# Software-pipelining the prefix state update of a gated linear attention kernel over (chunk, head) items

## The chip, the cores and the metric

The kernel runs on all 8 cores of one Trainium2 chip. The cores do not exchange data. The metric is the device time in microseconds (us) of the slowest core.

## The reference

One transformer layer: gated linear attention (GLA), then a mixture-of-experts FFN, each between a layer norm and a normed residual. The change touches the GLA only, cut here to its core (B = 2, S = 8192, D = 1024, H = 8, DK = 128, DV = 256):

```python
q, k, v = x @ Wq, (x @ Wk) * DK ** (-0.5), x @ Wv          # per head
alpha = sigmoid((x @ Wg + bg) / 16.0)                        # one per token and head
def step(state, inp):
    state = at[..., None, None] * state + kt[..., None] * vt[:, :, None, :]
    out_t = jnp.einsum('bhk,bhkv->bhv', qt, state)
out = outs * sigmoid(x @ Wog) @ Wo
```

## The kernel before

**Split.** Each core owns 2048 tokens of one batch row. The state at the first of them depends on all tokens before, so each core first runs a *prefix* of 6144 tokens (filled up with zeros where fewer exist) that only builds the state, and then the mixer for its own tokens, and then the FFN. All cores do the same amount of work.

**Prefix** (`emit_prefix`). 12 super-tiles of 512 tokens, each with: the load of `x_tm` (issued by SyncE once the previous super-tile's gate work is done), layer norm and transposes (VectorE, ScalarE, TensorE), the K and V projections (long rows of matmuls into banks 2 and 3), the gate (`emit_gproj`, `emit_gateprep`, which end with `Rxb` and `Rxm`, the exponentials of running sums of log alpha), and then the state updates: 4 chunks of 128 tokens x 8 heads = 32 *items* (c, h), in that order, one call of `emit_state_update` each. That makes 12 x 32 = 384 items.

**One item i** has seven steps. The letters are used throughout; `par` is h % 2 and picks one of two SBUF buffers.

- B(i), TensorE: two matmuls that spread the head's row of `Rxb` and `Rxm` over 128 partitions, into bank 6 (`pb<-Rxb,isel8b` and `pb<-Rxm,isel8b`)
- K(i), VectorE, L536: `khb` = k times the second of them
- E(i), ScalarE, L541: `expB`, one column of the first (the decay of the chunk)
- T(i), TensorE: transpose of `khb` into bank 7 (`pb<-iI128b,khb`)
- C(i), ScalarE, L547: copy of it to SBUF, `khT`
- S(i), TensorE: the state's increment, `khT` x `v_tm`, into another part of bank 7 (`pb<-v_tm,khT`)
- A(i), VectorE, L555: `S_state` = `S_state` x `expB` + bank 7

**What sets the order.** Each engine runs its instructions in the order of the program, and waits at semaphores that the helpers place. `mm` (start of a group in a bank) waits until all readers recorded for that bank have finished, whatever part of the bank they read; `pbread` (a read of a bank) waits for the last sealed matmul of that bank, and enters itself as a reader. `opi` on VectorE and ScalarE adds a wait for that engine's own previous instruction. A wait that an earlier, later-counting wait on the same semaphore already covers is left out (`Bld.wait`). All matmuls are issued by L158, in `mm`.

Of the kernel before, what the change touches and what calls it, by code (L numbers as in the profile page):

```python
# [11 lines left out]
ALU = mybir.AluOpType  # L12
# [3 lines left out]
H, DK, DV, D, HDV = 8, 128, 256, 1024, 2048  # L16
C = 128
# [130 lines left out]
def mm(b, pb, out, lhsT, rhs, start, stop, seal=False):  # L148
    if start:
        assert not pb.open, "interleaved accumulation groups in one PSUM bank"  # L150
        for tok in pb.rtoks:
            b.wait("t", tok)
        pb.rtoks = []
        pb.open = True
    if stop:
        pb.open = False
    pb.unsealed = True
    fn = lambda E, o=out, l=lhsT, r=rhs, st=start, sp=stop: E.matmul(  # L158
        o, l, r, start=st, stop=sp)
    if seal:  # L160
        pb.wtok = b.opi("t", fn)
        pb.unsealed = False
    else:
        b.op("t", fn)


def pbread(b, pb, e, fn):
    assert not pb.unsealed, "reading PSUM bank with unsealed writes"
    b.wait(e, pb.wtok)
    tok = b.opi(e, fn)  # L170
    pb.rtoks.append(tok)
    return tok
# [34 lines left out]
def _build(cfg, dma_plan):  # L207
# [51 lines left out]
    b = Bld(nc, es, dma_plan)  # L259
    _dbgn = [0]  # L260

    def dkey():
        _dbgn[0] += 1
        return "dbg%d" % _dbgn[0]
# [3 lines left out]
    pb = [PB(es.enter_context(nc.psum_tensor(f"pb{i}", [128, 512], F32)))  # L268
          for i in range(8)]
    iI128b = sb("iI128b", [128, 128], BF16)  # L270
    iones1b = sb("iones1b", [1, 128], BF16)
    iones2b = sb("iones2b", [2, 128], BF16)
    CCm = TS // C
    expB_rd = [None, None]
# [31 lines left out]
    isel8b = msb("isel8b", [8, 8 * 128], BF16)  # L306
    imask = msb("imask", [128, 128], F32)
    S_state = msb("S_state", [128, H * DV], F32)
# [7 lines left out]
    Rxb = msb("Rxb", [8, TS], BF16)  # L316
    Rxm = msb("Rxm", [8, TS], BF16)
# [5 lines left out]
    khb = [msb(f"khb{p}", [128, 128], BF16) for p in range(2)]  # L323
    khT = [msb(f"khT{p}", [128, 128], BF16) for p in range(2)]
    Sbf = [msb(f"Sbf{p}", [128, DV], BF16) for p in range(2)]
    expB_sb = [msb(f"expB{p}", [128, 1], F32) for p in range(2)]
    outog = msb("outog", [128, 16, 128], BF16)
    xln_fm = msb("xln_fm", [128, 8, TS], BF16)
    k_fm = msb("k_fm", [128, H, TS], BF16)
    v_tm = msb("v_tm", [128, CCm, H * DV], BF16)  # L330
# [24 lines left out]
    def emit_ln1(x_src_3d, cc, st_off=0):  # L355
        o = st_off
        for j in range(cc):
            sqb = sqbuf[j % 2]
            b.opi("v", lambda E, j=j: E.reduce_sum(  # L359
                st_s1[:, o + j:o + j + 1], x_src_3d[:, j, :], axis=AX.X))  # L360
            b.wait("s", sq_rd[j % 2])
            tsq = b.opi("s", lambda E, j=j, sqb=sqb: E.activation(
                sqb[:, :], x_src_3d[:, j, :], AF.Square))
            b.wait("v", tsq)
            sq_rd[j % 2] = b.opi("v", lambda E, j=j, sqb=sqb: E.reduce_sum(  # L365
                st_sq[:, o + j:o + j + 1], sqb[:, :], axis=AX.X))
        b.wait("s", b.tok("v"))
        b.opi("s", lambda E, o=o, cc=cc: E.mul(
            st_mean[:, o:o + cc], st_s1[:, o:o + cc], 1.0 / D))
        tmsq = b.opi("s", lambda E, o=o, cc=cc: E.activation(  # L370
            st_msq[:, o:o + cc], st_mean[:, o:o + cc], AF.Square))
        b.wait("v", tmsq)
        tvar = b.opi("v", lambda E, o=o, cc=cc: E.scalar_tensor_tensor(
            st_var[:, o:o + cc], st_sq[:, o:o + cc], 1.0 / D, st_msq[:, o:o + cc],
            ALU.mult, ALU.subtract))
        b.wait("s", tvar)
        b.wait("s", tk_eps)
        b.op("s", lambda E, o=o, cc=cc: E.activation(
            st_msq[:, o:o + cc], st_var[:, o:o + cc], AF.Ln,
            bias=ieps[:, :], scale=1.0))  # L380
        tkr = b.opi("s", lambda E, o=o, cc=cc: E.activation(
            st_rstd[:, o:o + cc], st_msq[:, o:o + cc], AF.Exp, bias=0.0, scale=-0.5))
        b.wait("v", tkr)
        tmr = b.opi("v", lambda E, o=o, cc=cc: E.scalar_tensor_tensor(
            st_mr[:, o:o + cc], st_mean[:, o:o + cc], -1.0, st_rstd[:, o:o + cc],
            ALU.mult, ALU.mult))
        b.wait("s", tmr)
        return tmr
# [137 lines left out]
            Rxm[:, 0:cc * C], ts2[:, 0:cc * C], AF.Exp, bias=0.0, scale=1.0))  # L526
        return tkR, None

    def emit_state_update(c, h, par, tkR, v_tok):
        bank6 = pb[6]  # L530
        b.wait("t", tkR)
        mm(b, bank6, bank6.sl(par * 256, 128), isel8b[:, h * 128:(h + 1) * 128],
           Rxb[:, c * C:(c + 1) * C], start=True, stop=True)
        mm(b, bank6, bank6.sl(par * 256 + 128, 128), isel8b[:, h * 128:(h + 1) * 128],
           Rxm[:, c * C:(c + 1) * C], start=True, stop=True, seal=True)
        tkh = pbread(b, bank6, "v", lambda E, bank6=bank6, par=par, c=c, h=h: E.tensor_tensor(  # L536
            khb[par][:, :], k_fm[:, h, c * C:(c + 1) * C],
            bank6.sl(par * 256 + 128, 128), ALU.mult))
        b.wait("s", expB_rd[par])
        b.wait("s", tkh)  # L540
        tEB = pbread(b, bank6, "s", lambda E, bank6=bank6, par=par: E.copy(  # L541
            expB_sb[par][:, :], bank6.sl(par * 256 + 127, 1)))
        bank7 = pb[7]
        b.wait("t", tkh)
        mm(b, bank7, bank7.sl(par * 128, 128), khb[par][:, :], iI128b[:, :],
           start=True, stop=True, seal=True)
        tkt = pbread(b, bank7, "s", lambda E, bank7=bank7, par=par: E.copy(  # L547
            khT[par][:, :], bank7.sl(par * 128, 128)))
        b.wait("t", tkt)
        if v_tok is not None:  # L550
            b.wait("t", v_tok)
        mm(b, bank7, bank7.sl(256, 256), khT[par][:, :],
           v_tm[:, c, h * DV:(h + 1) * DV], start=True, stop=True, seal=True)
        b.wait("v", tEB)
        tadd = pbread(b, bank7, "v", lambda E, bank7=bank7, par=par, h=h: E.scalar_tensor_tensor(  # L555
            S_state[:, h * DV:(h + 1) * DV], S_state[:, h * DV:(h + 1) * DV],
            expB_sb[par][:, :], bank7.sl(256, 256), ALU.mult, ALU.add))
        expB_rd[par] = tadd
        return tadd

    x_cons = [None]
    x_par = [0]
# [1 line left out]
    def emit_prefix():  # L564
        for s in range(n_pre_st):
            if x_cons[0] is not None:
                b.wait("y", x_cons[0][0])
                b.wait("y", x_cons[0][1])
            tkx = b.dma("y", x_tm[:, :, :],
                        x_pre.rearrange("(a p) n -> p a n", p=128)[:, s * CCm:(s + 1) * CCm, :],  # L570
                        "x%d" % (x_par[0] % 2))
            x_par[0] += 1
            b.wait("v", tkx)
            b.wait("s", tkx)
            emit_ln1(x_tm, CCm)
            for j in range(CCm):
                tkn = emit_norm_sub(x_tm, j, xlnbuf[j % 2])
                emit_transpose_to_fm(xlnbuf[j % 2], xln_fm, tkn, j * 128)
            tk_fmdone = b.tok("s")
            x_cons[0] = (b.tok("v"), b.tok("s"))  # L580
            if cfg.micro < 2:
                continue
            b.wait("t", tk_fmdone)
            b.wait("t", tk_wk)
            b.wait("t", tk_wv)
            b.wait("t", tk_wg)
            def kev(bank, i, n0, nn):
                pbread(b, bank, "v", lambda E, bank=bank, i=i, n0=n0, nn=nn: E.tensor_copy(
                    k_fm[:, i, n0:n0 + nn], bank.sl(0, nn)))
            proj_fm_resident(k_fm, Wk_sb, H, TS, kev, scale_tok=tk_wks)  # L590
            v_tok = emit_vproj(CCm, TS)
            if cfg.micro < 3:
                x_cons[0] = (b.tok("v"), b.tok("s"))
                continue
            tk_la = emit_gproj(CCm, TS)
            x_cons[0] = (b.tok("v"), b.tok("s"))
            if cfg.micro < 4:
                continue
            tkR, _ = emit_gateprep(CCm, tk_la)
            x_cons[0] = (b.tok("v"), b.tok("s"))  # L600
            if cfg.micro < 8:
                continue
            for c in range(CCm):
                for h in range(H):
                    emit_state_update(c, h, h % 2, tkR, v_tok)
        if cfg.debug:
            tkf = b.tok("v")
            b.wait("y", tkf)
            tdS = b.dma("y", dbg["dbg_S"][:, :], S_state[:, :], dkey())
            for _e in ("t", "v", "s"):  # L610
                b.wait(_e, tdS)
# [201 lines left out]
    def emit_ffn():  # L813
# [308 lines left out]
        ffn_es.close()  # L1122

    emit_prefix()
    pre_es.close()
    if cfg.stop_after != "prefix":
# [120 lines left out]
```

How the kernel before makes its waits and increments, by code:

```python
    def opi(self, e, fn):  # L76
        h, n = self.sem[e]
        if e in self.AUTO_SER and n > self.waited[e].get(e, 0):
            self.waited[e][e] = n
            self.emit(e, lambda E, h=h, c=n: E.wait_ge(h, c))
        self.sem[e][1] += 1
        self.emit(e, lambda E, fn=fn, h=h: fn(E).then_inc(h, 1))
        return (e, self.sem[e][1])
# [4 lines left out]
    def wait(self, e, tok):  # L88
        if tok is None:
            return
        pe, cnt = tok
        if pe == e and e not in self.AUTO_SER:
            return
        if self.waited[e].get(pe, 0) >= cnt:
            return
        self.waited[e][pe] = cnt
        h = self.sem[pe][0]
        self.emit(e, lambda E, h=h, c=cnt: E.wait_ge(h, c))
# [3 lines left out]
    def dma(self, qe, out, in_, skey):  # L102
        if skey not in self.sem:
            self._mksem(skey)
            self.dma_keys.add(skey)
        idx = self.dma_calls.get(skey, 0)
        self.dma_calls[skey] = idx + 1
        amt = 16
        if self.dma_plan is not None:
            amt = self.dma_plan[skey][idx]
        self.sem[skey][1] += amt
        h = self.sem[skey][0]
        self.emit(qe, lambda E, o=out, i=in_, h=h: E.dma_start(
            out=o, in_=i).then_inc(h, 16))
        return (skey, self.sem[skey][1])
```

## Time and profile before

| | us |
|---|---|
| runs shown | 7725.72 and 7847.7 (median 7786.71) |
| profiled execution, device time | 7743.92 |
| its span, first to last instruction, slowest core (core 3) | 7742.4 |
| spans of the eight cores | 7695.7 to 7742.4 |
| core 3: TensorE busy | 4506.5 (58%) |
| core 3: VectorE busy | 2088.2 (27%) |
| core 3: ScalarE busy | 1576.8 (20%) |

The profile is one execution, seen on the slowest core. On core 3 the prefix ends near 1982 us, the core's own tokens near 3800 us, and the FFN takes the rest. Busy shares are averages over these parts. In the timelines, each line is one instruction: start, duration, engine, line, operation, and in brackets how long the engine was idle before it and what released it.

### The profile page before, as it was taken

What the parts mean: (1) busy time and instruction counts of PE and PEld (TensorE: products, weight loads), DVE (VectorE), ACT (ScalarE), POOL (GpSimd) and SP (SyncE); (2) the same over time, 40 slices, a digit from 0 to 9 for tenths busy, and PEclk for the clock granted to TensorE, in tenths of its full rate; (3) what the DMA queues carried; (4) which work ended last, traced back from release to release, by engine and by line L of the source; (5) the groups of instructions that cost most, each with busy time, mean ns of one, the idle gap of its engine ahead of it and who ended that gap; (6) DMA issues with size and microseconds to landing.
All of it is one profiled execution on the core that took longest, in us unless ns stands there. A gap on an engine that the chain in (4) does not pass through costs nothing.

```text
span 7742.4 us, 71715 instructions; the slowest of 8 cores (7695.7 to 7742.4 us)
## 1 busy us (share of the span) xinstructions
PE 4506.5 (58%) x21600; PEld 2075.7 (27%) x21600; DVE 2088.2 (27%) x4478; ACT 1576.8 (20%) x3527; POOL 246.9 (3%) x300
## 2 busy tenths in 40 slices
PE   3455444554544535454305777777777777778880
PEld 1122221222221212222102333333333333334440
DVE  2333333333222232322342122222222222221113
ACT  1221222212122111212221122222222222221112
POOL 0000000000100001000000000000000000000000
PEclk8667666666666757576557899999999999999985
DMA  2000000000411304031003111111211111112102
GB/s 55 11 11 12 22 11 11 11 11 11 63 22 30 33 20 44 9 40 21 27 25 46 22 22 22 22 22 26 37 26 22 22 22 22 22 22 44 22 1 84
DMA packets 265487, 200.18 MB, mean 26 GB/s; under 512 B 142020, under 2 KB 224068, under 8 KB 265110
## 3 DMA queue, kind: packets, MB, share of 16 engines
q0 software_dynamic: 244448, 128.23, 12.7%
q1 hardware_dynamic: 20662, 67.36, 2.5%
q8 instruction: 183, 3.00, 0.2%
q14 instruction: 194, 1.59, 0.1%
HBM read 307.00 MB, written 16.78 MB: 42 GB/s over the span
## 4 chain that ended last, share of the span: by engine, by line
PE 54%; ACT 15%; DVE 13%; issue 11%; DMA 5%; ACTq 1%; DVEq 1%; POOL 0%; POOLq 0%; SPq 0%
PE pb L158 54%; ACT h_sc L1041 4%; DVE S_state L555 2%; ACT cwb_sb L1023 2%; DVE st_sq L365 2%; DVE st_s L359 2%; DMA wog_buf<-Wog 2%; DVE khb L536 1%; ACT khT L547 1%; ACT xln_fm L406 1%; DMA wq_buf<-Wq 1%; DMA wk_buf<-Wk 1%; ACT Sbf L750 1%; DMA y<-y_sb 1%; ACT xlnB L391 1%
## 5 line engine op out<-in xcount | busy, mean ns | idle before, releaser
L158 PE MATMUL pb<-x1ln_fm,w1g 128*128 128x384 bf16 (+1 forms) x7680 | 1354.6, 323 | 728.3 <-ACT h_sc L1041 408.6
L158 PE MATMUL pb<-w2g,h_sc 128*128 128x512 bf16 x5120 | 1202.2, 387 | 8.9 <-DVE h_sc L1048 8.9
L158 PEld LDWEIGHTS pb<-x1ln_fm,w1g 128*128 128x128 bf16 x7680 | 681.0, 101 | 1348.8 <-issue 1036.3
L1048 DVE TENSOR_TENSOR h_sc<-h_sc,cwb_sb 128x384 bf16<-128x384 bf16 (+1 forms) x768 | 258.1, 336 | 2029.6 <-ACT h_sc L1041 1987.9
L1041 ACT ACTIVATE h_sc<-pb,b1T_sb 128x384 bf16<-128x384 f32 (+1 forms) x768 | 420.1, 547 | 1323.7 <-PE pb L158 1323.7
L158 PEld LDWEIGHTS pb<-w2g,h_sc 128*128 128x128 bf16 x5120 | 506.9, 100 | 592.5 <-issue 71.7
L1082 DVE TENSOR_TENSOR acc<-acc,pb 128x512 f32<-128x512 f32 x640 | 439.9, 687 | 669.2 <-PE pb L158 614.9
L158 PE MATMUL pb<-Wv_sb,xln_fm 128*128 128x512 bf16 x2048 | 444.6, 379 | 0.0
L1023 ACT CAST cwb_sb<-pb 128x384 bf16<-128x384 f32 (+1 forms) x384 | 170.7, 445 | 963.4 <-PE pb L158 924.5
L158 PE MATMUL pb<-v_tm,khT 128*128 128x256 bf16 x512 | 189.2, 370 | 289.1 <-ACT khT L547 217.2
L555 DVE SCALAR_TENSOR_TENSOR S_state<-S_state,expB,pb 128x256 f32<-128x256 f32 x384 | 184.3, 480 | 587.2 <-PE pb L158 587.2
L158 PE MATMUL pb<-iI128b,khb 128*128 128x128 bf16 x512 | 141.9, 277 | 335.7 <-DVE khb L536 335.7
L158 PE MATMUL pb<-iI128b,xlnA 128*128 128x128 bf16 x320 | 40.5, 306 | 489.2 <-ACT xlnA L391 489.2
L158 PEld LDWEIGHTS pb<-Wv_sb,xln_fm 128*128 128x128 bf16 x2048 | 200.2, 98 | 241.8
L462 DVE CAST v_tm<-pb 128x512 bf16<-128x512 f32 x256 | 177.1, 692 | 264.9 <-PE pb L158 264.9
L158 PE MATMUL pb<-smb,v_tm 128*128 128x128 bf16 x256 | 61.1, 288 | 305.2 <-ACT Sbf L750 305.2
L158 PE MATMUL pb<-xln_fm,Wk_sb 128*128 128x512 bf16 x768 | 199.1, 428 | 14.0 <-ACT xln_fm L406 14.0
L541 ACT COPY expB<-pb 128x1 f32<-128x1 f32 x384 | 61.8, 161 | 674.5 <-DVE khb L536 658.2
L1041 ACT ACTIVATE h_sc<-pb,sb1T_sb 128x384 bf16<-128x384 f32 (+1 forms) x192 | 105.0, 547 | 455.4 <-PE pb L158 451.8
L158 PE MATMUL pb<-xln_fm,wog_buf 128*128 128x512 bf16 x512 | 142.1, 432 | 91.2 <-DMA wog_buf<-Wog 86.0
L158 PE MATMUL pb<-cwT,selg 64*128 64x384 bf16 (+1 forms) x384 | 126.5, 329 | 97.0 <-DVE selg L1007 70.9
L158 PEld LDWEIGHTS pb<-iI128b,khb 128*128 128x128 bf16 x512 | 58.8, 115 | 426.8 <-issue 426.8
(145 smaller groups left out, 3757.0 us busy)
## 6 DMA issues: line engine op xcount, KB each, us to landing
w1g<-w POOLq DMA_DIRECT2D x64, 512.0 KB, 13.8
w2g<-w POOLq DMA_DIRECT2D x64, 512.0 KB, 15.6
x_tm<-x_pre SPq DMA_DIRECT2D x12, 2048.0 KB, 9.0
wog_buf<-Wog POOLq DMA_DIRECT2D x64, 256.0 KB, 4.4
x_tm<-x_own SPq DMA_DIRECT2D x4, 2048.0 KB, 7.6
wq_buf<-Wq POOLq DMA_DIRECT2D x32, 256.0 KB, 5.2
wk_buf<-Wk POOLq DMA_DIRECT2D x32, 256.0 KB, 5.1
x_sp<-x_tm SPq DMA_DIRECT2D x16, 512.0 KB, 2.6
```

The costliest lines, as they stand in the source:

```text
L158: fn = lambda E, o=out, l=lhsT, r=rhs, st=start, sp=stop: E.matmul(o, l, r, start=st, stop=sp)
L359: b.opi("v", lambda E, j=j: E.reduce_sum(st_s1[:, o + j:o + j + 1], x_src_3d[:, j, :], axis=AX.X))
L365: sq_rd[j % 2] = b.opi("v", lambda E, j=j, sqb=sqb: E.reduce_sum(st_sq[:, o + j:o + j + 1], sqb[:, :], axis=AX.X))
L391: return b.opi("s", lambda E, j=j, dst=dst: E.activation(dst[:, :], x_src_3d[:, j, :], AF.Identity, bias=st_mr[:, st_off + j:st_off + j + ...
L406: pbread(b, bank, "s", lambda E, bank=bank, half=half: E.copy(dst_fm[:, half * 4:half * 4 + 4, tslice0:tslice0 + 128], bank.t[:, 0:512].re ...
L462: pbread(b, bank, "v", lambda E, bank=bank, c=c, cb4=cb4: E.tensor_copy(v_tm[:, c, cb4 * 512:(cb4 + 1) * 512], bank.t[:, 0:512]))
L536: tkh = pbread(b, bank6, "v", lambda E, bank6=bank6, par=par, c=c, h=h: E.tensor_tensor(khb[par][:, :], k_fm[:, h, c * C:(c + 1) * C], ban ...
L555: tadd = pbread(b, bank7, "v", lambda E, bank7=bank7, par=par, h=h: E.scalar_tensor_tensor(S_state[:, h * DV:(h + 1) * DV], S_state[:, h * ...
L1023: lambda E, bankh=bankh, par=par, tscnt=tscnt: E.copy(cwb_sb[:, par, 0:tscnt], bankh.sl(0, tscnt)))
L1041: dst=dst, tscnt=tscnt: E.activation(dst[:, par, hc, 0:tscnt], bankh.sl(0, tscnt), AF.Silu, bias=bias_ap, scale=1.0))
L1048: b.op("v", lambda E, par=par, hc=hc, tscnt=tscnt: E.tensor_tensor(h_sc[:, par, hc, 0:tscnt], h_sc[:, par, hc, 0:tscnt], cwb_sb[:, par, 0: ...
L1082: lambda E, bank=bank, g128=g128, half=half: E.tensor_tensor(acc[:, g128, half * 512:(half + 1) * 512], acc[:, g128, half * 512:(half + 1) ...
```

## The change

`emit_state_update` is replaced by `emit_prefix_scan`, which emits the 32 items of a super-tile together, in three groups of steps: `front(i)` = B, K, E; `mid(i)` = T, C; `back(i)` = S, A. Round i of the loop emits front(i), then mid(i-1), then back(i-2). So each engine's program order in a round becomes

- TensorE: B(i), T(i-1), S(i-2)
- VectorE: K(i), A(i-2)
- ScalarE: E(i), C(i-1)

After the last round come mid(31), back(30), back(31). The banks, the two buffers of `khb`, `khT` and `expB`, and every instruction's operands are the same as before. `khb_rd` is a new guard: K(i) waits for T(i-2). E(i) is ordered after A(i-4) and not after A(i-2), so that the `expB` buffer of item i-2 is written again before A(i-2) reads it.

```diff
-    def emit_state_update(c, h, par, tkR, v_tok):
-        (B, K, E, T, C, S, A of one item, in this order)
+    khb_rd = [None, None]
+
+    def emit_prefix_scan(cc, tkR, v_tok):
+        bank6, bank7 = pb[6], pb[7]
+        seq = [(c, h) for c in range(cc) for h in range(H)]
+        st_f = {}
+        def front(i):
+            c, h = seq[i]
+            par = i % 2
+            b.wait("t", tkR)
+            mm(b, bank6, bank6.sl(par * 256, 128), isel8b[:, h * 128:(h + 1) * 128],
+               Rxb[:, c * C:(c + 1) * C], start=True, stop=True)
+            mm(b, bank6, bank6.sl(par * 256 + 128, 128), isel8b[:, h * 128:(h + 1) * 128],
+               Rxm[:, c * C:(c + 1) * C], start=True, stop=True, seal=True)
+            b.wait("v", khb_rd[par])
+            tkh = pbread(b, bank6, "v", ...khb...)
+            b.wait("s", expB_rd[par])
+            b.wait("s", tkh)
+            tEB = pbread(b, bank6, "s", ...expB_sb...)
+            st_f[i] = (tkh, tEB)
+        def mid(i):
+            par = i % 2
+            tkh, tEB = st_f[i]
+            b.wait("t", tkh)
+            mm(b, bank7, bank7.sl(par * 128, 128), khb[par][:, :], iI128b[:, :],
+               start=True, stop=True, seal=True)
+            khb_rd[par] = ("t", b.sem["t"][1])
+            tkt = pbread(b, bank7, "s", ...khT...)
+            st_f[i] = (tkt, tEB)
+        def back(i):
+            c, h = seq[i]
+            par = i % 2
+            tkt, tEB = st_f.pop(i)
+            b.wait("t", tkt)
+            if v_tok is not None:
+                b.wait("t", v_tok)
+            mm(b, bank7, bank7.sl(256, 256), khT[par][:, :],
+               v_tm[:, c, h * DV:(h + 1) * DV], start=True, stop=True, seal=True)
+            b.wait("v", tEB)
+            tadd = pbread(b, bank7, "v", ...S_state...)
+            expB_rd[par] = tadd
+        n = len(seq)
+        for i in range(n):
+            front(i)
+            if i >= 1:
+                mid(i - 1)
+            if i >= 2:
+                back(i - 2)
+        if n >= 1:
+            mid(n - 1)
+        if n >= 2:
+            back(n - 2)
+        if n >= 1:
+            back(n - 1)
...
-            for c in range(CCm):
-                for h in range(H):
-                    emit_state_update(c, h, h % 2, tkR, v_tok)
+            emit_prefix_scan(CCm, tkR, v_tok)
```

## Rows read from the trace of the kernel before

**Rows 1.** The page: its head, the busy line, the granted clock.

```profile
span 7742.4 us, 71715 instructions; the slowest of 8 cores (7695.7 to 7742.4 us)
...
PE 4506.5 (58%) x21600; PEld 2075.7 (27%) x21600; DVE 2088.2 (27%) x4478; ACT 1576.8 (20%) x3527; POOL 246.9 (3%) x300
...
PEclk8667666666666757576557899999999999999985
```

**Rows 2.** Busy time by stretch: state updates, the work between them, state updates again.

```profile
core 3: us, PE busy (x) PEld busy (x) DVE busy (x) ACT busy (x) POOL busy (x), PEclk, DMA share, GB/s
...
139.00:216.50 77.50, 30.63 (x128) 10.63 (x128) 24.57 (x64) 14.76 (x65) 0.00 (x0) 0.50 0.08 28
216.50:300.00 83.50, 52.43 (x242) 24.97 (x242) 29.86 (x44) 19.08 (x26) 0.00 (x0) 0.77 0.00 1
300.00:377.00 77.00, 30.28 (x126) 10.50 (x126) 24.58 (x65) 14.79 (x66) 0.00 (x0) 0.50 0.08 28
```

**Rows 3.** Chain of work by time, 302.4 to 308: start, duration, what.

```profile
304.38 0.49 DVE S_state L555
304.87 0.03 issue
304.90 0.02 DVEq L80
304.92 0.04 issue
304.97 0.30 DVE khb L536
305.27 0.14 issue
305.40 0.28 PE pb L158
```

**Rows 4.** Timeline of one item and the start of the next.

```profile
304.97 0.29 DVE L536 TENSOR_TENSOR khb<-k_fm,pb 128x128 bf16<-128x128 bf16 x1
...
305.40 0.27 PE L158 MATMUL pb<-iI128b,khb 128*128 128x128 bf16 x1 [0.89 <-DVE khb L536]
305.45 0.16 ACT L541 COPY expB<-pb 128x1 f32<-128x1 f32 x1 [1.77 <-DVE khb L536]
305.81 0.27 ACT L547 CAST khT<-pb 128x128 bf16<-128x128 f32 x1 [0.20 <-PE pb L158]
...
306.23 0.37 PE L158 MATMUL pb<-v_tm,khT 128*128 128x256 bf16 x1 [0.56 <-ACT khT L547]
...
306.53 0.28 PE L158 MATMUL pb<-Rxb,isel8b 8*128 8x128 bf16 x1
...
306.61 0.31 PE L158 MATMUL pb<-Rxm,isel8b 8*128 8x128 bf16 x1
306.77 0.48 DVE L555 SCALAR_TENSOR_TENSOR S_state<-S_state,expB,pb 128x256 f32<-128x256 f32 x1 [1.51 <-PE pb L158]
307.35 0.29 DVE L536 TENSOR_TENSOR khb<-k_fm,pb 128x128 bf16<-128x128 bf16 x1
```

**Rows 5.** Instructions that write khT and expB over the whole run.

```profile
L547 ACT CAST khT<-pb x384: 266/267/267, 140.5 to 1979.7; 128x128 bf16<-128x128 f32 x192
...
L541 ACT COPY expB<-pb x384: 161/161/162, 140.2 to 1979.3; 128x1 f32<-128x1 f32 x192
```

**Rows 6.** Timeline, own tokens: ScalarE's next instruction behind the expB copy.

```profile
2188.53 0.16 ACT L745 COPY expB<-pb 128x1 f32<-128x1 f32 x1 [1.51 <-DVE khb L740]
2188.78 0.41 ACT L750 CAST Sbf<-S_state 128x256 bf16<-128x256 f32 x1
```

**Rows 7.** Timeline where a super-tile's state updates begin.

```profile
139.12 0.26 PE L158 MATMUL pb<-Rxb,isel8b 8*128 8x128 bf16 x1 [1.30 <-ACT Rxm L525]
...
139.66 0.29 DVE L536 TENSOR_TENSOR khb<-k_fm,pb 128x128 bf16<-128x128 bf16 x1 [1.46 <-PE pb L158]
```

**Rows 8.** Timeline where they end and the next layer norm begins.

```profile
375.81 2.21 ACT L362 ACTIVATE sq<-x_tm 128x1024 f32<-128x1024 f32 x2
...
376.41 0.48 DVE L555 SCALAR_TENSOR_TENSOR S_state<-S_state,expB,pb 128x256 f32<-128x256 f32 x1 [1.51 <-PE pb L158]
376.99 1.22 DVE L359 TENSOR_REDUCE st_s<-x_tm 128x1 f32<-128x1024 f32 x1
```

**Rows 9.** Timeline of an item with a late khT copy.

```profile
322.11 0.27 PE L158 MATMUL pb<-iI128b,khb 128*128 128x128 bf16 x1 [0.87 <-DVE khb L536]
322.16 0.16 ACT L541 COPY expB<-pb 128x1 f32<-128x1 f32 x1 [1.76 <-DVE khb L536]
322.58 0.27 ACT L547 CAST khT<-pb 128x128 bf16<-128x128 f32 x1 [0.25 <-PE pb L158]
```

More of the change, by code:

```diff
@@ L527, in emit_gateprep @@
         return tkR, None
-    def emit_state_update(c, h, par, tkR, v_tok):
[L530 to L559, printed above, removed]
@@ new lines, in _build @@
+    khb_rd = [None, None]
[12 more added lines that the diff above has]
+            b.wait("v", khb_rd[par])
+            tkh = pbread(b, bank6, "v", lambda E, par=par, c=c, h=h: E.tensor_tensor(
+                khb[par][:, :], k_fm[:, h, c * C:(c + 1) * C],
+                bank6.sl(par * 256 + 128, 128), ALU.mult))
+            b.wait("s", expB_rd[par])
+            b.wait("s", tkh)
+            tEB = pbread(b, bank6, "s", lambda E, par=par: E.copy(
+                expB_sb[par][:, :], bank6.sl(par * 256 + 127, 1)))
+            st_f[i] = (tkh, tEB)
[6 more added lines that the diff above has]
+            khb_rd[par] = ("t", b.sem["t"][1])
+            tkt = pbread(b, bank7, "s", lambda E, par=par: E.copy(
+                khT[par][:, :], bank7.sl(par * 128, 128)))
+            st_f[i] = (tkt, tEB)
[9 more added lines that the diff above has]
+            b.wait("v", tEB)
+            tadd = pbread(b, bank7, "v", lambda E, par=par, h=h: E.scalar_tensor_tensor(
+                S_state[:, h * DV:(h + 1) * DV], S_state[:, h * DV:(h + 1) * DV],
+                expB_sb[par][:, :], bank7.sl(256, 256), ALU.mult, ALU.add))
+            expB_rd[par] = tadd
[12 more added lines that the diff above has]
+            back(n - 1)
```

## Prediction

> **What bounds the kernel now.** I read the page first. TensorE is busy 58% of the span and no other engine reaches 30% [rows 1], and the granted clock is low through the first half. So the prefix is not at the rate of any engine, and the busy shares say nothing about the change. Next I cut the prefix into stretches [rows 2]. The state updates of a super-tile fill a stretch of about 77 us in which TensorE is busy 30 us, VectorE 25 us and ScalarE 15 us, at a granted clock of 0.50 (the 1.2 GHz level). Between two such stretches the clock averages 0.77. Twelve stretches of 77 us are some 920 us, 12% of the span: this is all that the change touches. No engine is full in it, so latency sets it.
>
> The chain of waits shows which latency [rows 3], and the timeline gives each step [rows 4]. K starts at 304.97 and the next K at 307.35: one item takes 2.38 to 2.40 us; I use 2.39. From start to start the hand-overs in the loop are:
>
> - A(i-1) to K(i): 304.38 to 304.97, 0.59 (the VectorE instruction of 0.48 and 0.11 for the wait on itself)
> - K(i) to T(i): 304.97 to 305.40, 0.43
> - T(i) to C(i): 305.40 to 305.81, 0.41
> - C(i) to S(i): 305.81 to 306.23, 0.41 to 0.42
> - S(i) to A(i): 306.23 to 306.77, 0.55
>
> Their sum is 2.39. All seven steps lie in one line except E (305.45 to 305.61, beside T) and B (306.53 to 306.92, beside A). The durations of the two ScalarE steps do not vary over 384 items [rows 5]. At the end of the stretch the next layer norm starts on VectorE 0.58 after the last A began [rows 8], while ScalarE has gone ahead. So the end of the last A sets when the next stage begins, and what the stretch loses the run loses.
>
> **The change, step by step.** Nothing is removed: the same seven steps of each item run, on the same two banks. What changes is who stands behind whom. I follow a steady round from the start of S(i-2), with what stands ahead of each instruction:
>
> 1. A(i-2) needs S(i-2): +0.55.
> 2. K(i+1) is next on VectorE and waits for its own engine: +0.59 more. Its B(i+1) was issued behind S(i-2), 0.31 to 0.69 after its start as in [rows 4], and is done in time.
> 3. E(i+1) starts 0.48 after K(i+1) (304.97 to 305.45 [rows 4]). Its three waits are the ones it has now.
> 4. T(i) needs bank 7 free of A(i-2), and K(i) long done. VectorE to TensorE takes 0.14 [rows 3], so T(i) starts 0.62 after A(i-2) began, at about the time K(i+1) starts. It is ready for C(i) at 0.62 + 0.41 = 1.03 after A(i-2) began.
> 5. C(i) stands behind E(i+1) on ScalarE. E(i+1) starts 0.59 + 0.48 = 1.07 after A(i-2), takes 0.16, and then comes ScalarE's wait on itself. Before, that hand-over is hidden, since T ends later. The nearest row is on the core's own tokens, where the same 0.16 us copy is followed at once by another ScalarE instruction: 2188.53 + 0.16 to 2188.78 is 0.09 [rows 6]. So C(i) starts at 1.07 + 0.16 + 0.09 = 1.32, not at 1.03. T is off the path with 0.29 to spare.
> 6. S(i-1) needs bank 7 free of C(i), which is the reader just entered, although its own operand C(i-1) has been ready for a round: +0.41.
>
> The round is 0.55 + 0.59 + 0.48 + 0.25 + 0.41 = 2.28 us. Before it was 0.55 + 0.59 + 0.43 + 0.41 + 0.41 = 2.39. The whole gain of a round is that E with its hand-overs (0.48 + 0.25 = 0.73) takes the place of T with its own (0.43 + 0.41 = 0.84): 0.11 us. The three-deep order on paper overlaps nothing else, because bank 7 is shared by T, C, S and A, and `mm` waits for every reader of the bank.
>
> Filling and draining have to be paid once per super-tile. I count from K(0), which starts 0.54 after B(0) [rows 7] in both kernels.
>
> Before: A(31) starts at 31 x 2.39 + 0.43 + 0.41 + 0.42 + 0.55 = 75.9 and ends at 76.4. (The stretch shown ran from 300.17 to 376.89, 76.7; the rest is scattered late issues such as [rows 9], which I leave alike in both.)
>
> After: E(0) ends at 0.64; B(1) must wait for it (0.14), and K(1) follows at 0.78 + 0.54 = 1.32. By the same step K(2) starts at 2.64, E(2) at 3.12, C(1) at 3.37, S(0) at 3.78, A(0) at 4.33. Then 29 rounds of 2.28: A(29) starts at 70.45. The tail: T(31) at +0.62 = 71.07, C(31) 71.48, S(30) 71.89, A(30) 72.44, then S(31) again at +0.62 = 73.06, A(31) 73.61, ended 74.1.
>
> 76.4 - 74.1 = 2.3 us for each super-tile, and 12 x 2.3 = 27 us. The profiled execution took 7743.9 us, so the forecast is **7716.5 us**, 0.35% less. The runs of before shown have a median 43 us above their profiled execution (0.6%), more than the whole effect. What a comparison of this kernel can tell from no change is about 2%.
>
> *Costs at nothing.* TensorE gets two more waits per item (B now waits for K of the item before, S for two copies in place of one). Both are met before the instruction ahead has finished, so they lie under S and under C. A met wait costs about 0.06 in the chain (0.02 and 0.04 [rows 3]); if the cover were gone, 2 x 0.06 x 384 = 46 us would turn the gain into a loss of 19 us. The new guard on `khb` and the one on `expB` emit nothing, as later waits on the same semaphores cover them. No DMA is moved: the load of the next x tile is issued by SyncE before the first item and is not on this chain. If E were late, C, S, A and the next K behind it all move.
>
> *A page on this.* The Trainium skill says in PSUM — Partial Sum Buffer, "PSUM bank collisions raise a hardware error", that two engines must not touch one bank in the same partitions at once, other columns or not, so that semaphores should guard whole banks. That is a rule against the overlap the new order seems to offer. It agrees with the trace, where T, C, S and A follow each other strictly.
>
> **The rivals.**
>
> *Bank 7 alone sets the round.* If C did not queue behind E (say E started much earlier than it does now), the loop would be T 0.41, C 0.41, S 0.55, A 0.62 = 1.99 us. That is 0.29 less than 2.28, over 29 rounds and 12 super-tiles 101 us more gained: 7616 us. Against it: E(i+1) is emitted before C(i), ScalarE runs in order, and E cannot start before K. Chance 0.03.
>
> *Full overlap.* If the items really overlapped three deep, TensorE would be the bound with 0.28 + 0.31 + 0.27 + 0.37 = 1.23 us an item [rows 4]. 384 x (2.39 - 1.23) = 445 us: 7298 us, 5.7% less. For it: TensorE is busy only 30 of 77 us [rows 2]. Against it: the bank's readers, above. Chance 0.03.
>
> *The clock rises.* TensorE does the same work in 3% less time, 30 us in 74 in place of 30 in 77. Of its steps only S, 0.37, lies on the new loop together with its share of hand-overs. If the stretch ran at the 2.4 GHz level and S halved, 0.185 x 30 x 12 = 67 us more would be gained: 7650 us. Against it: 0.50 in both stretches shown [rows 2], and the density hardly changes. Chance 0.04.
>
> The Trainium skill, TensorE: Matmul & The Clock Gate, "What's actually happening", says that the throttled state is the default and sustained activity releases it, and under "Single matmul latency" it gives about 0.27 us warm for 256 columns against 0.40 cold (the trace has 0.37 at the low level). By that a released clock would be worth some 0.10 us a round, not 0.185: about 36 us, 7680 us.
>
> *Slower: ScalarE's hand-over from E to C.* This is the one term that before doesn't show in its place. The longest such gap in the stretch shown is 322.32 to 322.58, 0.26 [rows 9], though there T is named as the releaser. With 0.26 for 0.09 the round is 2.45, a super-tile takes 74.1 + 30 x 0.17 = 79.2, and the run 12 x 2.8 = 34 us more than now: 7778 us. The point from which it decides is a gap of 0.09 + 2.3 / 30 = 0.17. Chance 0.10. To lose over 2% (155 us) a round would have to cost 0.5 us more than forecast; no row speaks for that.
>
> **How the numbers follow.** The forecast's own case has 0.80 (7700 to 7735, by 0.04 on a round either way). The range reaches up to the slower case and a little past it, for the spread between runs, and down to the clock case: 7645 to 7790. It leaves out the two overlap cases and runs far up. Faster by over 2% (below 7589) is the full overlap and little else: 0.04. Slower by over 2%: 0.02, for a hand-over far past its bound. Within 2%: 0.94.
>
> **What would show it.** In the new profile K follows K by 2.28 us, T starts within 0.05 of the next K, the idle time before C is ended by something on ScalarE or by nothing the profile names rather than by TensorE, S starts 0.41 after C, and from a super-tile's first K to its last A's end it is 74.1 (plus a few tenths). If K follows K by 2.0 or less, step 5 is wrong; if T still comes 0.4 after the K of its own round, step 4 is; a clock above 0.50 in these stretches is the third rival. A stage outside the prefix that changes by more than a few us would mean that something other than the order of these steps acts.

## The result and the profile after

| | before | after |
|---|---|---|
| median of all runs, us | 7816.17 (42 runs) | 7775.18 (45 runs) |
| fastest run | 7718.31 | 7685.90 |
| ratio after / before | 1 | 0.9943, 95% interval 0.9916 to 0.997 |
| one super-tile's state updates, first K to last A's end | 76.8 | 74.6 |
| from a super-tile's first K to the next one's | 160.4 | 157.0 |
| K projection, super-tiles 2 to 12, mean | 16.3 | 15.3 |
| prefix, first K to last A's end | 1840.7 | 1802.8 |

The change makes the kernel faster by 0.57% (0.3 to 0.84%), 44 us by the ratio, where 27 us (0.35%) were forecast. The lower four rows are from the timelines of core 7 in the first profile of each kernel. In some executions some cores run at a lower clock for part of the time (four did in the first profile of the changed kernel): the ratio is over executions without that, such cores are left out in what follows, and the lines of the changed kernel below are from a second execution, without it, on its slowest core.

Its page, against [rows 1]: 7687.5 against 7742.4 us of span, and TensorE busy for 27 us less; the busy times of the other engines differ by at most 8 us.

```profile
span 7687.5 us, 72123 instructions; the slowest of 8 cores (7657.5 to 7687.5 us)
...
PE 4479.0 (58%) x21600; PEld 2068.3 (27%) x21600; DVE 2089.4 (27%) x4478; ACT 1572.1 (20%) x3527; POOL 247.2 (3%) x300
```

Busy time by stretch, against [rows 2] (state updates, the work between them, state updates; the columns are those of [rows 2]): the state updates take 74.6 us in place of 77, with the granted clock still at 0.50. So the clock did not rise in them.

```profile
140.20:214.90 74.70, 30.69 (x128) 10.69 (x128) 24.17 (x64) 15.35 (x66) 0.00 (x0) 0.50 0.08 29
214.90:297.90 83.00, 51.60 (x240) 24.71 (x240) 30.27 (x44) 18.37 (x26) 0.00 (x0) 0.77 0.00 1
297.90:372.50 74.60, 30.70 (x128) 10.70 (x128) 24.13 (x63) 15.15 (x66) 0.00 (x0) 0.50 0.08 29
```

The timeline of one round, against [rows 4] (VectorE L545 is K, L575 is A; ScalarE L550 is E, L561 is C):

```profile
302.29 0.37 PE L158 MATMUL pb<-v_tm,khT 128*128 128x256 bf16 x1 [1.07 <-ACT khT L561]
...
302.85 0.48 DVE L575 SCALAR_TENSOR_TENSOR S_state<-S_state,expB,pb 128x256 f32<-128x256 f32 x1 [1.41 <-PE pb L158]
303.43 0.29 DVE L545 TENSOR_TENSOR khb<-k_fm,pb 128x128 bf16<-128x128 bf16 x1
...
303.47 0.26 PE L158 MATMUL pb<-iI128b,khb 128*128 128x128 bf16 x1 [0.49 <-DVE S_state L575]
303.92 0.16 ACT L550 COPY expB<-pb 128x1 f32<-128x1 f32 x1 [1.77 <-PE pb L158]
304.16 0.27 ACT L561 CAST khT<-pb 128x128 bf16<-128x128 f32 x1
...
304.57 0.37 PE L158 MATMUL pb<-v_tm,khT 128*128 128x256 bf16 x1 [0.84 <-ACT khT L561]
```

S to S is 302.29 to 304.57, 2.28 us. The steps are S to A 0.56, A to K 0.58, K to E 0.49, E to C 0.24, C to S 0.41. T starts 0.04 after K and is no longer on the path; C has no idle time before it at all, since it stands right behind E, and bank 7 has the order T, C, S, A without overlap. (The releaser named before E is a matmul that had ended long before; what E waits for is K.)

The start and the end of a super-tile's state updates, against [rows 7] and [rows 8]:

```profile
140.80 0.29 DVE L545 TENSOR_TENSOR khb<-k_fm,pb 128x128 bf16<-128x128 bf16 x1 [1.46 <-PE pb L158]
...
142.13 0.29 DVE L545 TENSOR_TENSOR khb<-k_fm,pb 128x128 bf16<-128x128 bf16 x1 [1.05 <-PE pb L158]
...
143.46 0.29 DVE L545 TENSOR_TENSOR khb<-k_fm,pb 128x128 bf16<-128x128 bf16 x1 [1.05 <-PE pb L158]
...
144.60 0.37 PE L158 MATMUL pb<-v_tm,khT 128*128 128x256 bf16 x1 [1.07 <-ACT khT L561]
```

```profile
213.67 0.48 DVE L575 SCALAR_TENSOR_TENSOR S_state<-S_state,expB,pb 128x256 f32<-128x256 f32 x1 [1.51 <-PE pb L158]
...
214.84 0.48 DVE L575 SCALAR_TENSOR_TENSOR S_state<-S_state,expB,pb 128x256 f32<-128x256 f32 x1 [0.69 <-PE pb L158]
215.43 1.22 DVE L359 TENSOR_REDUCE st_s<-x_tm 128x1 f32<-128x1024 f32 x1
```

K(1), K(2) and S(0) come 1.33, 2.66 and 3.80 after K(0), and A(31) starts 1.17 after A(30): fill and drain are as forecast to 0.02.

**Where the rest came from.** On core 7, the twelve stretches of state updates take 922.2 us before and 895.7 after, 26.5 less. The eleven stretches between them, in which the program is the same, take 918.4 and 907.1, 11.3 less. Of these 11.3, 11.0 are in the K projection, the first long row of matmuls (179.7 us before and 168.7 after, summed over super-tiles 2 to 12, from its first matmul to the first of the V projection). Super-tile 8, first before (core 7), then after (core 0):

```profile
1203.20 16.72 PE L158 MATMUL pb<-xln_fm,Wk_sb 128*128 128x512 bf16 x64 [1.12 <-ACT xln_fm L406]
1219.75 5.56 PE L158 MATMUL pb<-Wv_sb,xln_fm 128*128 128x512 bf16 x25
```

```profile
1185.49 15.59 PE L158 MATMUL pb<-xln_fm,Wk_sb 128*128 128x512 bf16 x64 [1.12 <-ACT xln_fm L406]
1200.92 4.26 PE L158 MATMUL pb<-Wv_sb,xln_fm 128*128 128x512 bf16 x19
```

The same 64 matmuls take 16.55 and 15.43 us. Busy time in steps of 2 us from their start shows why: the third column from the right is the granted clock. Before:

```profile
1203.20:1205.20 2.00, 2.00 (x5) 0.69 (x6) 0.00 (x0) 0.00 (x0) 0.00 (x0) 0.50 0.03 8
1205.20:1207.20 2.00, 2.00 (x6) 0.73 (x5) 0.26 (x1) 0.00 (x0) 0.00 (x0) 0.50 0.00 0
1207.20:1209.20 2.00, 2.00 (x7) 0.70 (x6) 0.43 (x1) 0.00 (x0) 0.00 (x0) 0.60 0.00 0
1209.20:1211.20 2.00, 2.00 (x11) 0.93 (x10) 0.69 (x1) 0.00 (x0) 0.00 (x0) 1.00 0.00 0
```

After:

```profile
1185.50:1187.50 2.00, 2.00 (x5) 0.68 (x6) 0.00 (x0) 0.00 (x0) 0.00 (x0) 0.50 0.00 0
1187.50:1189.50 2.00, 2.00 (x8) 0.76 (x7) 0.33 (x1) 0.00 (x0) 0.00 (x0) 0.68 0.00 0
1189.50:1191.50 2.00, 2.00 (x11) 0.94 (x10) 0.97 (x2) 0.00 (x0) 0.00 (x0) 1.00 0.04 8
```

The projection starts at the 1.2 GHz level in both kernels and is raised to 2.4 GHz while it runs: 5.6 us after its start before (4 us, and the 2 us step at 0.60 has a fifth of its time high), 3.3 us after its start in the changed kernel. About 2.3 us less at half speed give half of that back, 1.1 us, eleven times.

### The profile page after: what moved, and what is told of

Same layout as the page of the kernel before. It is cut to its first block, busy times and chain, and to the rows that moved or that the text cites. A ratio compares the mean times of both kernels' runs of the same rounds, so it can differ in the third digit from the quotient of the medians.

```text
span 7845.3 us, 71807 instructions; the slowest of 8 cores (7670.4 to 7845.3 us)
## 1 busy us (share of the span) xinstructions
PE 4587.4 (58%) x21284; PEld 2105.5 (27%) x21600; DVE 2089.0 (27%) x4478; ACT 1572.1 (20%) x3527; POOL 246.9 (3%) x300
## 4 chain that ended last, share of the span: by engine, by line
PE 53%; ACT 15%; DVE 13%; issue 11%; DMA 5%; ACTq 1%; DVEq 1%; POOL 0%; POOLq 0%; SPq 0%
PE pb L158 53%; ACT h_sc L1072 4%; DVE S_state L575 2%; ACT cwb_sb L1054 2%; DVE st_s L359 2%; DVE st_sq L365 2%; DMA wog_buf<-Wog 2%; DVE khb L545 1%; ACT khT L561 1%; ACT xln_fm L406 1%; ACT expB L550 1%; DMA wq_buf<-Wq 1%; DMA wk_buf<-Wk 1%; DMA y<-y_sb 1%; ACT Sbf L781 1%
## 5 line engine op out<-in xcount | busy, mean ns | idle before, releaser
L158 PE MATMUL pb<-x1ln_fm,w1g 128*128 128x384 bf16 (+1 forms) x7680 | 1411.0, 333 | 726.2 <-ACT h_sc L1072 407.7
L575 DVE SCALAR_TENSOR_TENSOR S_state<-S_state,expB,pb 128x256 f32<-128x256 f32 x384 | 184.6, 481 | 537.2 <-PE pb L158 537.2
L550 ACT COPY expB<-pb 128x1 f32<-128x1 f32 x384 | 61.2, 159 | 657.6 <-PE pb L158 607.3
L158 PEld LDWEIGHTS pb<-v_tm,khT 128*128 128x128 bf16 x512 | 53.6, 105 | 490.4 <-issue 490.4
```

The costliest lines, as they stand in the source:

```text
L550: tEB = pbread(b, bank6, "s", lambda E, par=par: E.copy(expB_sb[par][:, :], bank6.sl(par * 256 + 127, 1)))
L575: tadd = pbread(b, bank7, "v", lambda E, par=par, h=h: E.scalar_tensor_tensor(S_state[:, h * DV:(h + 1) * DV], S_state[:, h * DV:(h + 1) * ...
```

## The experiments

Twelve kernels ran. "Period" is the time from a super-tile's first K to the next one's, "prefix" that from the first K of all to the last A's end. Each row is from one core of the kernel's profile; the other cores give the same prefix within 3 us, except in `warm`. A period that alternates is given as a mean or as both values. K projection is the mean over super-tiles 2 to 12.

| kernel | round | state updates | K projection | period | prefix |
|---|---|---|---|---|---|
| before | 2.39 | 76.8 | 16.3 | 160.4 | 1840.7 |
| after | 2.28 | 74.6 | 15.3 | 157.0 | 1802.8 |
| exp4 | 2.27 | 74.6 | 15.3 | 157.0 | 1801.9 |
| delay_a | 2.28 | 74.6 | 15.6 and 16.7 in turn | 158 and 159 in turn | 1818.7 |
| delay_d | 2.28 | 74.7 | 15.7 | 160.5 | 1840.5 |
| warm (its fastest core) | 2.27 | 74.6 | 13.8 or 15.5 | 155.7 | 1787.6 |
| before_fill | 2.39 | 76.8 | 13.8 | 157.3 | 1807.4 |
| after_fill | 2.27 | 74.6 | 13.8 | 155.0 | 1779.6 |
| e_behind_c | 1.99 | 65.7 | 15.9 | 148.7 | 1701.4 |
| bank7_split | 1.33 | 45.3 | 15.9 | 128.3 | 1456.1 |
| all_split | 1.14 | 37.8 | 15.9 | 120.8 | 1366.9 |
| split_fill | 1.14 | 37.8 | 13.8 | 118.3 | 1339.3 |

### Is it the start of the projection that meets the clock elsewhere? (delay_a, delay_d)

One or four memsets on VectorE behind each super-tile's state updates:

```diff
             emit_prefix_scan(CCm, tkR, v_tok)
+            b.opi("v", lambda E: E.memset(yn_sb[:, 0:512], 0.0))
```

> The changed kernel with one extra VectorE memset (512 columns) behind the state updates of each of the 12 super-tiles, so that the next layer norm starts about 0.55 us later (estimated from the 128x2048 memset, 1.77 us, and 0.1 for the wait on itself). In the changed kernel the time from a super-tile's first K to the next one's is 157.01 us, and TensorE's first 3.2 us or so of the projections run at the 1.2 GHz level. Theory 1 (the clock's rise does not follow the start of the projection by a fixed time, so work that starts later meets the rise sooner): the period stays at 157.0, the slow stretch shrinks by about twice the delay, to about 2.1 us, and the prefix ends as before within 1 us. Theory 2 (the projections got faster for a reason that has nothing to do with when they start): the period becomes 157.6 and the prefix ends 6 to 7 us later.

```profile
L637 DVE MEMSET yn_sb<- x12: 485/485/485, 213.5 to 1957.6; 128x512 f32 x12
```

With its hand-overs a memset delayed the layer norm by 0.73 us (last A to layer norm 1.31 in place of 0.58), a little more than expected. The period is neither 157.0 nor 157.7: it alternates (157.9, 159.3, 158.1, 159.4, 158.3 in a row on core 1, though not to the end: 157.4, 158.8 and 158.0 follow), and with it the K projection. Two super-tiles one after the other:

```profile
1034.68 15.82 PE L158 MATMUL pb<-xln_fm,Wk_sb 128*128 128x512 bf16 x64 [1.12 <-ACT xln_fm L406]
```

```profile
1192.99 16.87 PE L158 MATMUL pb<-xln_fm,Wk_sb 128*128 128x512 bf16 x64 [1.12 <-ACT xln_fm L406]
```

The prefix is 1816.2 to 1818.7 us on cores 0 to 5, 14 to 16 us longer, for 11 x 0.73 = 8.0 us of added delay. So neither theory had the number, but the second falls: with the same program from the memset on, the projections take two different times in turn, and the loss is nearly twice the delay. The first keeps its mechanism and loses its claim that a small delay is free.

> The same with four such memsets, about 2.2 us in each super-tile, which gives back nearly all that the new order of the state updates saves in one (2.3 us by the timeline). Theory 1 (the clock): the period goes back to the 160.4 of the kernel before, 3.4 us for 2.2 paid, the slow stretch at the start of the projections to about 5 us, and the prefix ends near 1978 us. Theory 2 (no clock effect): the period is 159.2 and the prefix ends near 1966 us.

The four memsets delayed the layer norm by 2.9 us, not 2.2, since each has 0.24 us of idle time before it. The period is 160.5, that of the kernel before, and steady; the prefix is 1840.5, again that of before, and the K projection is at 15.7. By adding alone it would be 157.0 + 2.9 = 159.9 and 1834.8. The difference has the right sign but is small, so this run alone would prove little. That the period fell on the 160.4 that was expected is in part luck, since the delay was mis-sized (2.9 us for 2.2); and the K projection did not go back to the 16.3 of the kernel before.

### Taking the clock's part out of both kernels (warm, before_fill, after_fill)

Matmuls whose result is not used, between the transposes; in `warm` 5, 5, 5 and 2 of them, in the two others:

```diff
                 emit_transpose_to_fm(xlnbuf[j % 2], xln_fm, tkn, j * 128)
+                if s >= 1:
+                    for _f in range((5, 6, 8, 4)[j]):
+                        mm(b, pb[0], pb[0].sl(0, 512), iI128b[:, :],
+                           Wv_sb[:, 0, 0:512], start=True, stop=True)
```

> The changed kernel with extra TensorE work whose result is not used: from the second super-tile on, five matmuls of 512 columns behind the transposes of each of the first three token blocks and two behind the last, so that TensorE is busy before the projections begin. Theory 1 (part of the gain is clock: what TensorE does at the 1.2 GHz level at the start of the K projection): the clock is up at the start, the 64 matmuls of the K projection take about 14.0 in place of 15.64 us, and up to 11 x 1.6 = 18 us are gained if the extra matmuls are hidden under ScalarE's 2.46 us between transposes. Theory 2: the K projection stays at 15.6 us.

The prefix is 9 to 15 us shorter than in the changed kernel, by core. The K projection takes 13.81 us in three to seven of the eleven super-tiles, by core, and 15.2 to 15.5 in the others. So `warm` supports the cause, but on most cores it has the clock up in time in fewer than half of the super-tiles.

> The kernel before, with extra matmuls of 512 columns on TensorE between the transposes of each super-tile from the second on (5, 6, 8 and 4 of them behind the four blocks; their result is not used), so that the clock is up before the K projection begins whatever the phase. If the clock is the only thing that differs outside the state updates, the K projection takes 13.8 us here (16.4 before), the period falls from 160.4 to about 157.8 and the prefix ends some 28 us earlier than in the kernel before. If the projections have another cause for their time, they stay above 15 us.

> The same extra matmuls in the changed kernel. Theory (clock): K projection 13.8 us (15.3 without), period about 155.5, and the prefix now ends only the state updates' own saving earlier than in the kernel before with the same extra matmuls: 12 x 2.2 = 27 us, where without them the two differ by 38 us. Rival (the new order itself shortens the projections): the two differ by 38 us here too.

Both have a K projection of 13.81 us in every super-tile from the second on. That of the eighth, before_fill with its first 2 us (granted clock 1.00 from the start), and then after_fill:

```profile
1186.78 13.97 PE L158 MATMUL pb<-xln_fm,Wk_sb 128*128 128x512 bf16 x64 [0.46 <-ACT xln_fm L406]
...
1186.80:1188.80 2.00, 2.00 (x10) 0.93 (x11) 0.00 (x0) 0.00 (x0) 0.00 (x0) 1.00 0.00 0
```

```profile
1171.40 13.97 PE L158 MATMUL pb<-xln_fm,Wk_sb 128*128 128x512 bf16 x64 [0.46 <-ACT xln_fm L406]
```

Now the stretches between the state updates are alike (885.2 and 884.6 us in all), and the two prefixes differ by 27.8 us, where without the extra matmuls it is 37.9 (medians over the cores: 27.2 and 38.1). That is the forecast's 12 x 2.3 = 27. The rest of the gain was the clock.

### What holds the round (exp4, e_behind_c, bank7_split, all_split)

> The changed kernel with four expB buffers in place of two, so that E(i) no longer overwrites the decay that A(i-2) has still to read; E(i) waits for A(i-4). That wait is long met. If the round is K, E, C, S, A as read from the trace, it stays at 2.28 us and the run's time does not change. If the reuse of the buffer had let something run early, the round gets longer.

The edit gives `expB_sb` four buffers, indexed by i % 4, and `b.wait("s", expA.get(i - 4))` for the guard. The round is 2.27 to 2.28, the prefix 1801.9: the reuse of the buffer had no part in the time. This is the form to use. In the changed kernel as it stands E(i+1) writes the buffer that A(i-1) has still to read (303.92 in the timeline above, before even S(i-1) at 304.57), so A(i-1) decays the state by the factor of the item two places on. That isn't the reference's recurrence, and two more buffers of one column put it right at no cost in time.

In e_behind_c, front(i) is only B and K, and E is emitted behind mid:

```diff
             front(i)
             if i >= 1:
                 mid(i - 1)
+            late(i)          # E(i)
             if i >= 2:
                 back(i - 2)
```

> The changed kernel with ScalarE's order in a round turned round: C(i-1) first, then E(i); expB has four buffers, each read before it is written again. If the round of 2.28 us is set by K, E and C on the way from one A to the next S, the round becomes that of bank 7 alone, T 0.41 + C 0.41 + S 0.55 + A 0.62 = 1.99 us, and the state updates of a super-tile take about 66 us in place of 74.5. If something else holds the round (the wait of VectorE or TensorE between B and K), it stays at 2.28 or gets longer, since E then stands behind C.

```profile
301.16 0.27 ACT L567 CAST khT<-pb 128x128 bf16<-128x128 f32 x1 [1.48 <-PE pb L158]
301.51 0.16 ACT L556 COPY expB<-pb 128x1 f32<-128x1 f32 x1
...
301.57 0.37 PE L158 MATMUL pb<-v_tm,khT 128*128 128x256 bf16 x1 [0.56 <-ACT khT L567]
...
303.56 0.37 PE L158 MATMUL pb<-v_tm,khT 128*128 128x256 bf16 x1 [0.56 <-ACT khT L567]
```

S to S is 1.99, to the hundredth, and C is now released by T. So E, one column of 0.16 us in front of C, cost 0.29 us of every round of the changed kernel. The one run took 7619.0 us against 7736.6 of the kernel before on the same chip.

In bank7_split, T and C move to bank 0, which the prefix left unused:

```diff
-            mm(b, bank7, bank7.sl(par * 128, 128), khb[par][:, :], iI128b[:, :],
+            mm(b, bankT, bankT.sl(par * 128, 128), khb[par][:, :], iI128b[:, :],
...
-                khT[par][:, :], bank7.sl(par * 128, 128)))
+                khT[par][:, :], bankT.sl(par * 128, 128)))
```

> The changed order with T and C in bank 0, which the prefix does not use, and S and A left in bank 7; four expB buffers. If the shared bank 7 is what kept the items from overlapping (S(i-1) must wait for C(i), T(i) for A(i-2)), the round falls to the next loop, which is bank 6: B(i) to K(i) 0.54, K(i) to E(i) 0.48, E(i) to B(i+1) 0.30 = 1.32 us, and the state updates of a super-tile take some 45 us in place of 74.5: about 350 us less in the run. If the bank is not the reason, the round stays near 2.28, or falls no further than 2.0.

```profile
285.31 0.26 PE L158 MATMUL pb<-Rxb,isel8b 8*128 8x128 bf16 x1 [0.48 <-ACT expB L551]
...
285.85 0.29 DVE L546 TENSOR_TENSOR khb<-k_fm,pb 128x128 bf16<-128x128 bf16 x1 [0.37 <-PE pb L158]
...
286.34 0.16 ACT L551 COPY expB<-pb 128x1 f32<-128x1 f32 x1 [0.82 <-PE pb L158]
...
286.64 0.26 PE L158 MATMUL pb<-Rxb,isel8b 8*128 8x128 bf16 x1 [0.44 <-ACT expB L551]
```

B, K, E and the next B: 0.54 + 0.49 + 0.30 = 1.33 us, and B waits for E, as expected. One run of it took 7352.5 us. The shared bank is what made the three-deep order worth 0.11 us a round and not 1.06. (No run gave the old order a second bank; there T, C, S and A of an item wait for each other by their operands in any case.)

In all_split, `bank6, bank7, bankT = B6[par], B7[par], BT[par]` with banks 4 and 5, 6 and 7, 0 and 1.

> As bank7_split, and every one of the three uses has two banks that alternate: B in 4 and 5, T in 0 and 1, S in 6 and 7. Then no bank couples neighbouring items, and the round is that of VectorE: K and A with their waits on themselves, 0.29 + 0.11 + 0.48 + 0.11 = 0.99 us; a super-tile's state updates take some 35 us, the run is about 460 us (6%) shorter than the kernel before. Rival: TensorE's four matmuls follow each other without overlap at the 1.2 GHz level, 1.23 us by their busy times, and the round is not shorter than that (about 370 us less in the run).

Three rounds give a ratio to the kernel before of 0.9366 (0.9313 to 0.9419), 6.3% less, with the fastest run at 7252.4 us. A super-tile's state updates take 37.8 us. The round was mis-sized, 0.99 for a measured 1.14 (K follows K by 0.99 and 1.29 in turn; 1.15 with the late issues).

```profile
262.22 0.29 DVE L547 TENSOR_TENSOR khb<-k_fm,pb 128x128 bf16<-128x128 bf16 x1
262.71 0.16 ACT L552 COPY expB<-pb 128x1 f32<-128x1 f32 x1 [0.48 <-DVE khb L547]
262.93 0.48 DVE L579 SCALAR_TENSOR_TENSOR S_state<-S_state,expB,pb 128x256 f32<-128x256 f32 x1 [0.41 <-ACT expB L552]
262.96 0.27 ACT L564 CAST khT<-pb 128x128 bf16<-128x128 f32 x1
...
263.37 0.37 PE L158 MATMUL pb<-v_tm,khT 128*128 128x256 bf16 x1
263.51 0.29 DVE L547 TENSOR_TENSOR khb<-k_fm,pb 128x128 bf16<-128x128 bf16 x1
263.92 0.48 DVE L579 SCALAR_TENSOR_TENSOR S_state<-S_state,expB,pb 128x256 f32<-128x256 f32 x1
264.50 0.29 DVE L547 TENSOR_TENSOR khb<-k_fm,pb 128x128 bf16<-128x128 bf16 x1
```

VectorE is not full: it is idle for 0.41 us before every other A. I read this as the old chain, now over two items. From K(i) at 262.22 to E(i), C(i-1), S(i-1), A(i-1) and K(i+2) at 264.50 it is 0.49 + 0.25 + 0.41 + 0.55 + 0.58 = 2.28, and two rounds are 2.28. (The releaser named before A is another item's E; what A waits for by this reading is its own S.) The steps fit; no run tested it (E behind C with all banks split would). TensorE's 1.23 us, the rival bound, is undercut too: its matmuls' recorded durations overlap.

> The two-banks-each version together with the extra matmuls: the fastest form that the runs point to. The K projection falls from about 15.8 to 13.8 us in 11 super-tiles, 22 us, so about 7235 us in place of 7255, 0.3% less, if the extra matmuls stay hidden under ScalarE; no gain if the phase of the clock leaves the first of them slow and they hold up the transposes.

The two together: ratio 0.9342 (0.9269 to 0.9415), fastest run 7234.7 us. The K projection is 13.81 us in each super-tile from the second on. The fastest runs differ by 18 us in the expected direction, but the intervals of the two ratios overlap, so this part is seen in the prefix and not proved in the whole.

### Is the rest of the run touched? (before_again, after_again)

exp4 had shown 1800 to 1821 us for the core's own tokens, where the first profile of before had 1787 to 1807. These times run from the prefix's last K to the last K of all, and not from the first K of that part, as the expectation has it.

> The kernel before once more, for a second set of eight cores. The prefix, from a core's first K to its last, should take 1838 to 1845 us again. Open is the part for a core's own tokens (from the first K of that part to the last), which took 1787 to 1807 us in the first profile and 1804 to 1821 us in the run with four expB buffers: if that is spread between executions, this run may show up to 1820 us too; if the new order of the prefix costs the next part something, this run shows 1787 to 1807 us again.

> The changed kernel once more, with paired times. From first to last K of the prefix 1797 us, the period 157.0 us, the run 33 to 38 us below the kernel before (ratio 0.9955). Own tokens: 1787 to 1807 us if the 1804 to 1821 us seen with four expB buffers was spread, about 1812 us if it belongs to the new order.

before_again: 1793 to 1825 us; after_again: 1790 to 1811. So that part scatters between cores and executions by more than 20 us in either kernel, and nothing of it belongs to the change. The prefix hardly scatters: from first K to last K 1838 to 1839 us on all eight cores of before_again and 1797 to 1798 on all of after_again. Over the eight cores the median span is 7716.1 in the first profile of before and 7681.6 in after_again, 34.5 less. The fastest of after_again's six runs took 7689.1 us, against 7729.3 for the kernel before beside it, 40 less.

## Why the prediction was right and where it was wrong

- **The bound and the round: right.** Step 1 to step 6 stand in the timeline with at most 0.01 us of difference each, and the new term, 0.09 us from E to C read on the core's own tokens [rows 6], measured 0.08. T is off the path, C stands behind E.
- **Fill and drain: right.** 2.3 us for each super-tile was forecast, 26.5 us for the twelve was measured on core 7 (27.5 forecast), and 27.8 between the two filled kernels.
- **Costs at nothing: right**, with a miscount. The trace has 396 more separate wait instructions on TensorE, about one an item (in front of B) and not two, and each step of the round still took what was forecast. The guard on `expB` costs nothing (exp4).
- **Wrong: "what the stretch loses the run loses", the term for the work between the stretches.** It was set to nothing, without a price or a rival, and it was -11.3 us. The forecast looked at [rows 2] for a rise of the clock *inside* the state updates, found 0.50 and stopped there. The same rows show 0.77 for the stretch between: a clock that rises somewhere in it. When the projection begins elsewhere in relation to that rise, it spends another time at 1.2 GHz (5.6 us before and 3.3 after, in the eighth super-tile). The sum should have been 27 plus an open term. Its bound on the side of a gain is 11 x 2.5 = 28 us, the whole slow part (16.3 us for the K projection before, 13.8 with the clock up from the start); delay_a shows that it can be a loss as well.
- **Blind with it: the list of signs.** It names a change of more than a few us in a stage outside the prefix, and the clock inside the state updates. It has none for the other stages of the prefix itself, and there the K projection took 11.0 us less. The cause was the clock, set off by the new order.
- **The chances.** The forecast was right in sign, and its 0.35% lies inside the measured interval of 0.3 to 0.84%, near its lower end; but the effect was called too small to be told from no change, and with 45 and 42 runs it is told apart. The whole run's ratio cannot tell 27 from 38 us; the traces do. That the interval still holds the forecast owes something to its width and nothing to the missing term.
- **The rivals.** Bank 7 alone, full overlap, a clock that rises in the state updates and a slow hand-over from E to C all did not occur. The first was priced rightly as what another kernel would do: 1.99 us a round was measured once E stood behind C. The second was near in size (5.7% less forecast, 6.3% measured in all_split) but not in its bound: the round went below TensorE's 1.23 us.

## What to carry to other kernels

Before believing a software pipeline on paper, follow one resource at a time around the loop: a bank whose readers all have to finish ties every stage that uses it together, and here one more bank was worth 0.95 us a round where the new order alone gave 0.11. On an in-order engine a small instruction put ahead of the one that others wait for costs its whole hand-over (0.16 us of work, 0.29 us a round). And where a stretch ahead of a long row of matmuls gets shorter, look at the granted clock at the start of that row: what the row pays there can change as well.

## What the runs showed of the hardware that was not expected

A loop with a fixed amount of work seems to lock to the clock's rises. In before_again and after_again the period settles at 160.4 and 157.0 us over eleven super-tiles. The cores come together on it: on cores 0, 1, 3, 5 and 7 of after_again the first K projection takes 15.4 to 16.8 us and the twelfth 15.4 on each, and in before_again 15.3 to 16.4 and then 16.5 on each. With 0.73 us added the period does not settle but changes between about 158 and 159.3, and costs 1.3 to 1.4 us a super-tile. With 2.9 added it settles at 160.5. So 2.2 us saved in the state updates gave 3.4, and 0.73 added cost 1.3 to 1.4. That it is a lock is read from these numbers; no run set the time of the rises itself. The Trainium skill says in TensorE: Matmul & The Clock Gate, "What's actually happening", that the chip's look at TensorE's activity runs free and does not start anew with the kernel's work; the kernel with one memset (delay_a) agrees, in which the same row of matmuls took 15.6 and 16.7 us in turn, as it met the rise at two different places.
